# Linear attention and a sparse expert layer on one core: the tile loop written out, and the output product one step later

## Time and profile before

| what | us |
| --- | --- |
| timed runs: median (lowest, highest) of three | 238.04 (237.97, 239.08) |
| profiled execution: span from first to last instruction | 247.9 |
| TensorE busy in the span | 163.8 (66%) |
| VectorE busy | 171.3 (69%) |
| GpSimd busy | 124.1 (50%) |
| ScalarE busy | 99.9 (40%) |

### The profile page before, as it was taken

One profiled execution on the slowest core, in us unless ns is written; L12 is line 12 of the kernel. 1 busy time (PEld: TensorE's weight loads), 2 busy tenths in 40 slices (PEclk: granted clock), 3 DMA queues, 4 the chain that ended last, 5 costly groups with the idle time before them and its releaser, 6 DMA issues.

```text
span 247.9 us, 3949 instructions
## 1 busy us (share of the span) xinstructions
PE 163.8 (66%) x768; PEld 115.4 (47%) x769; DVE 171.3 (69%) x535; ACT 99.9 (40%) x359; POOL 124.1 (50%) x114
## 2 busy tenths in 40 slices
PE   2986966979494886965530004999999889964260
PEld 1444534746352545554420002877687667753140
DVE  0599999999999999999669800655564555540571
ACT  3234444481245822476540001644554454530080
POOL 5763333444057566546577720246466445553380
PEclk9999799797989976897555555999999999999687
DMA  5649100020000101020112243022223222211932
GB/s 149 201 109 408 33 13 3 0 74 11 1 5 17 64 0 43 13 76 23 65 43 86 85 120 81 18 72 78 77 75 85 69 80 65 70 38 64 300 104 73
DMA packets 19198, 18.54 MB, mean 75 GB/s; under 512 B 2944, under 2 KB 16256, under 8 KB 19056
## 3 DMA queue, kind: packets, MB, share of 16 engines
q1 hardware_dynamic: 16880, 13.69, 18.6%
q0 software_dynamic: 2304, 4.69, 5.6%
HBM read 10.60 MB, written 6.73 MB: 70 GB/s over the span
## 4 chain that ended last, share of the span: by engine, by line
PE 30%; issue 26%; DVE 18%; SPq 6%; POOL 6%; DMA 5%; ACT 4%; DVEq 2%; POOLq 0%; ACTq 0%
PE bank L745 8%; DVE prod L1014 5%; PE bank L753 5%; PE bank L736 5%; PE bank L734 3%; POOL zbuf L501 3%; DVE num L1021 3%; PE bank L735 3%; PE bank L571 2%; DMA pl<-both 2%; SPq L421 2%; DVE qk L990 2%; PE bank L725 2%; ACT actT L954 1%; SPq L428 1%
## 5 line engine op out<-in xcount | busy, mean ns | idle before, releaser
L538 POOL DMA_INDIRECT both<-yout,zin x39 | 37.4, 960 | 44.1 <-DVE yout L1295 28.2
L483 POOL TENSOR_TENSOR kv<-v,qk 128x1152 f32<-128x1152 f32 x16 | 34.9, 2180 | 36.2 <-DVE qk L990 32.0
L584 PE MATMUL bank<-kv,C 128*128 128x432 f32 (+1 forms) x96 | 39.8, 556 | 1.9 <-DVE prod L1014 1.8
L501 POOL DMA_INDIRECT zbuf<-rows,slot x32 | 32.1, 1004 | 13.8 <-issue 8.1
L745 PE MATMUL bank<-w_l,actT 128*128 x156 | 25.6, 286 | 7.0 <-ACT actT L954 6.4
L584 PEld LDWEIGHTS bank<-kv,C 128*128 128x128 f32 x96 | 20.2, 227 | 20.3 <-issue 16.1
L1295 DVE COPY yout<-bank 128x128 f32<-128x128 f32 x39 | 11.4, 292 | 24.7 <-PE bank L745 17.0
L745 PEld LDWEIGHTS bank<-w_l,actT 128*128 128x128 f32 x156 | 20.3, 190 | 17.4 <-issue 17.4
L725 PE MATMUL bank<-C,zin 128*128 128x128 f32 x39 | 11.3, 290 | 22.9 <-DMA zin<-zbuf 22.8
L1014 DVE TENSOR_TENSOR prod<-bank,qk 128x432 f32<-128x432 f32 (+1 forms) x48 | 24.4, 547 | 0.5 <-DVE slot L1178 0.5
L1280 DVE TENSOR_TENSOR zin_lo<-bank,zin_hi 128x128 fp32r<-128x128 f32 x39 | 11.4, 292 | 17.5 <-ACT zin_hi L944 14.2
(11 more groups left out here) (152 smaller groups left out, 359.8 us busy)
## 6 DMA issues: line engine op xcount, KB each, us to landing
zin<-zbuf SPq DMA_DIRECT2D x39, 65.0 KB
w_g<-in_gate_w SPq DMA_DIRECT2D x4, 512.0 KB, 6.3
pl<-both SPq DMA_DIRECT2D x8, 256.0 KB, 5.4
xTs<-in_xT SPq DMA_DIRECT2D x16, 64.0 KB, 2.2
w_l<-in_lin_w SPq DMA_DIRECT2D x1, 1024.0 KB, 9.4
zall<-zs SPq DMA_DIRECT2D x4, 256.0 KB
out<-pl SPq DMA_DIRECT2D x8, 128.0 KB, 1.8
both<-yout,zin POOLq DMA_INDIRECT x39
```

The lines of the kernel that those rows point to most:

```text
L483: pool.tensor_tensor(kv[:, s, :].rearrange("p (h e d) -> p h e d", e=HE, d=HD), a, b, ALU.mult).then_inc(kv_done, 1)
L501: pool.indirect_dma_start(zbuf, bass.IndirectOffsetOnAxis(ap=slot_of(g)[:, c:c + 1].bitcast(U32), axis=0), rows_of(g)[:, j, r, :], None)\
L538: pool.indirect_dma_start(both, bass.IndirectOffsetOnAxis(ap=zin[:, b, D + 1:D + 2].bitcast(U32), axis=0), yout[:, b, :], None).then_inc(p ...
L584: pe.matmul(pre_ps[b][:, 0:c1 - c0], const("tri"), kv[:, s, c0:c1], start=True, stop=True)\
```

## The change

The loop of `tiles` and the loops of SyncE and GpSimd over the tiles are written out, with constants as the values waited for. The stages `output` on TensorE and `take` on VectorE get lag 4 in place of 3. `output` also waits until the product of two tiles before, which used the same PSUM bank, has been taken. The expert's number is kept in eight registers in place of four, as it is needed for longer.

```diff
         def tiles(eng, *stages):
-            def step(k, n, rounds=0):
+            def step(k):
                 for lag, stage in stages:
-                    if not isinstance(k, int) or 0 <= k - lag < TILES:
-                        stage(k - lag, (n - lag) % BUFS, rounds + (n - lag) // BUFS)
-
-            for k in range(REST):
-                step(k, k)
-            with eng.Fori(0, ROUNDS) as i:
-                for b in range(BUFS):
-                    step(BUFS * i + (REST + b), REST + b, i)
-            for k in range(TILES, TILES + max(lag for lag, _ in stages)):
-                step(k, k)
+                    if 0 <= k - lag < TILES:
+                        stage(k - lag, (k - lag) % BUFS, (k - lag) // BUFS)
+
+            for k in range(TILES + max(lag for lag, _ in stages)):
+                step(k)
...
-            with sp.Fori(1, ROUNDS) as i:
-                for b in range(BUFS):
-                    k = BUFS * i + b
-                    sp.reg_load(row, tile_r[0:1, bass.ds(k, 1)])
-                    at = sp.snap(row, min_val=0, max_val=SPARE + (NSPARE - 1) * P)
-                    sp.wait_ge(placed[b], 16 * i)
-                    sp.dma_start(zin[:, b, :], zbuf[bass.ds(at, P), :]).then_inc(zin_loaded[b], 16)
-            for k in range(BUFS * ROUNDS, TILES):
-                b = k % BUFS
+            for k in range(BUFS, TILES):
+                rnd, b = divmod(k, BUFS)
                 sp.reg_load(row, tile_r[0:1, k:k + 1])
                 at_row = sp.snap(row, min_val=0, max_val=SPARE + (NSPARE - 1) * P)
-                sp.wait_ge(placed[b], 16 * ROUNDS)
+                sp.wait_ge(placed[b], 16 * rnd)
                 sp.dma_start(zin[:, b, :], zbuf[bass.ds(at_row, P), :]).then_inc(zin_loaded[b], 16)
...
-            with pool.Fori(0, ROUNDS) as i:
-                for b in range(BUFS):
-                    place(BUFS * i + b, b)
-            for k in range(BUFS * ROUNDS, TILES):
+            for k in range(TILES):
                 place(k, k % BUFS)
...
-            expert = [pe.alloc_register(f"expert{b}") for b in range(4)]
+            expert = [pe.alloc_register(f"expert{b}") for b in range(BUFS)]
...
             def output(k, b, rnd):
                 e = expert_of(b)
                 pe.wait_ge(actT_done, k + 1)
+                if k >= 2:
+                    pe.wait_ge(yout_done, k - 1)
...
-            tiles(pe, (0, turn_in), (1, gates), (3, output), (2, turn_act))
+            tiles(pe, (0, turn_in), (1, gates), (4, output), (2, turn_act))
...
-            tiles(ve, (0, rest_zin), (3, take), (1, activate))
+            tiles(ve, (0, rest_zin), (4, take), (1, activate))
```

More of the change, by code:

```diff
@@ L709, in _ @@
             ranks(last)
-            expert = [pe.alloc_register(f"expert{b}") for b in range(4)]
+            expert = [pe.alloc_register(f"expert{b}") for b in range(BUFS)]
             def look_up(k, b):
-                pe.reg_load(expert[b % 4], tile_e[0:1, at(k)])
+                pe.reg_load(expert[b % BUFS], tile_e[0:1, k:k + 1])
             def expert_of(b):
-                return pe.snap(expert[b % 4], min_val=0, max_val=E - 1)
+                return pe.snap(expert[b % BUFS], min_val=0, max_val=E - 1)
             def turn_in(k, b, rnd):
@@ L736, in gates @@
                 pe.matmul(g, zin_lo[:, b % 2, :], hi, start=False, stop=True).then_inc(gate_done, 1)
-                if not isinstance(k, int) or k + 1 < TILES:
+                if k + 1 < TILES:
                     look_up(k + 1, b + 1)
```

## The result

The changed kernel takes 251.53 us (median of four runs, 248.47 to 253.25), the kernel before 238.22 beside it. The ratio is 1.0481, with a 95% interval from 1.0422 to 1.054. The change makes the kernel slower, as was forecast, but by 13.3 us in the medians where 4.2 had been forecast, and 251.53 us lies above the stated range of 236.3 to 243.9. The ratio leaves out runs more than 1.5% above the fastest of their kernel, here 252.3 and 253.25, and the medians take them in, so the two do not divide exactly.

What follows compares the result with a forecast made beforehand. The ring of eight input buffers was to become the bound, four tiles per 6.5 us: stretch 52.0 against 48.0, +4.0, fill -0.45, drain +1.0, exit -0.3, so 238.04 + 4.2 = 242.2 us; range 236.3 to 243.9.

Steps and rivals of the forecast that it cites:

- The mechanism: Input buffers: reload waits for the scatter's landing, lag 4 lengthens the way round, TensorE waits for loads; 1.62 us per tile.
- few breaks: Steps where TensorE's signals come a microsecond late cost the first trace 9.3 us; timed runs were held likelier to have few.
- rival 1: Tiles 6 to 38: late-signal steps occur in timed runs too, so the change gains 1.7 us: 236.3 us; chance 0.27.
- the ring's turn: Way round the eight input buffers: 6.5 us besides whole steps, so after the change four tiles per 6.5 us.
- The load: Reload of an input buffer by SyncE: taken as 1.5 us, last packet plus its signal, between 0.9 and 1.83.
- The bound above: Ceiling of the input load, 1.83 us, from the first of eight loads in flight together; it would give +6.8 us.
- The restart: TensorE after waiting for a load: taken as a quiet step, 0.81 us transpose to output product, 0.64 to the take.
- The stretch before: Tiles 6 to 38 of the kernel before: 32 steps of 1.47 us plus 1.0 for loops, 48.0 us.
- Drain: Last tiles: scatters by GpSimd 1.30 us apart would make the end 1.0 us longer without breaks.
- fill: First steps: one output product moves out of step 3, saving 0.45 us.
- loops: Three ways back between tiles 6 and 38, 0.33 us each: writing out saves 1.0 us, plus 0.3 for the exit.
- The fourth rival: Input buffers: scatter and load both at about 2.15 us, so 7.03 us per four tiles, 246.4 us; chance 0.04.

Runs made afterwards that it cites:

- Experiments 1 to 6: Ratios to before: lag 4 only 1.0499; written out, lag 3, 8/7/6 buffers 1.0072/1.0535/1.1576; changed kernel with 12 buffers 0.99, or reloading before scatter lands 0.9917.
- experiment 2: The changed kernel with lag 3 instead of 4, loops still written out and added wait kept: 240.08 us, 1.0072 of before.
- experiment 0: The kernel before, unchanged, profiled a second time: span 238.7 us, timed at 240.61 us (one run).
- experiments 1 and 4: The kernel before with only lag 4, added wait and eight registers: 250.3 us; the changed kernel with lag 3 and 7 buffers: 250.74 us.
- experiment 4: The changed kernel with lag 3 and 7 buffers instead of lag 4 and 8: 250.74 us, 1.0535 of before.

## Why the prediction was right and wrong

**The mechanism was right.** The reload is bound to the scatter's landing, the lag lengthens the way round by a step, and TensorE waits at the input's transpose. Experiments 1 to 6 show it, and no other part of the change is shown to cost anything; the 0.7% of experiment 2 stays open.

**That the timed runs have few breaks was right,** though the evidence was thin: two numbers of like size, 9.3 and 9.9 us. No run of before reached 242 us, and experiment 0 has no break, so nothing speaks for rival 1. For the reason I gave, a profiler that delays signals, nothing speaks either; that the guess on the timed runs came true is in part luck.

**The step that failed: the ring's turn was mis-sized, 6.5 us against 7.17.** Term by term, by the chain of the changed kernel:

- The load: 1.5 against 1.87. I read a strip of the DMA engines up to the last packet and allowed next to nothing for the signal behind it. The bound above, 1.83, lay nearer. This is 0.37.
- The restart: I let a step that had waited run as a quiet one. From transpose to output product it takes 0.99 instead of 0.81, and its product 0.1 longer. From the transpose to the take it is 162.87 - 161.08 = 1.79 us where I had 0.81 + 0.64 = 1.45. This is 0.34. I had the 0.1 in the earlier trace rows and used it for the breaks, not for the ring.
- Scatter (2.23) and take to issue (0.30 + 0.03 + 0.74 = 1.07) were as read.

Eight turns are 57.4 us instead of 52.0: 5.4 us.

**Slow transfers had no term.** 61.66 - 57.4 = 4.3 us are turns longer than 7.17. Three reloads on the chain are 0.6, 1.7 and 1.4 us over 1.84, 3.7 in all, and nearly all of that is lost; the turn at the lower clock behind one of them is the other 0.9. The size differs from run to run: with the same spare steps experiments 1 and 4 have 60.47 and 60.32 in the stretch. With time to spare in the ring such a transfer costs little, as in the kernels with ten and twelve buffers; with none it adds nearly its whole lateness. I had a first scatter-to-reload of 3.04 in the earlier trace rows and put it only in a rival. Why a transfer is slow, no run shows.

**The stretch before was too cheap, by 2.2 us in the profile.** I took 48.0 us for tiles 6 to 38 of before; experiment 0 has 50.16. With the true turn the ring of before has 8 x 1.47 - 3 x 1.47 - (7.17 - 0.34) = 0.5 us to spare, not 0.9, so slow transfers reach it too. In experiment 0 the scatter and load of tile 8's buffer were 1.57 late together, some 1.05 more than there was to spare, and the step from tile 7 to tile 8 took 162.09 - 159.56 = 2.53 us, 1.05 over the quiet one. That is what 10 or 12 buffers win. This error had the other sign. Together: +5.4 + 4.3 - 2.2 = +7.5 on the +4.0 forecast for the stretch, the 11.5 measured. How the 13.3 us of the timed medians divide is not shown to that detail: the profiled run of before was one of its longer ones, and the 2.2 may be less in a usual run.

**Drain, fill and loops.** The drain grew from 6.97 to 7.95 us, +1.0 as predicted, by scatters 1.26 apart (I had 1.30). The transpose of tile 6 came 8.6 us after that of tile 0 instead of 9.8, but that is no measure of the change: it is 8.78 in the first profile of before, and over all profiles with at least 8 buffers 8.78 to 9.79 with lag 3 and 8.62 to 9.21 with lag 4, 0.4 apart in the mean where I had 0.45. The three ways back of the loop, 1.0 forecast, are steps 0.33, 0.27 and 0.23 longer in experiment 0, 0.8 together; no gain from writing them out is seen in the timed runs.

**The fourth rival came nearest.** It priced both transfers at about 2.15, an estimate by the Trainium skill (DMA: Bandwidth & Descriptors, anatomy of one DMA), and its turn of 7.03 us gave 246.4 us. I gave it 0.04 as the trace seemed to have the load at 1.5. The measured scatter is 2.2 and the load 1.8 to 1.9 in both kernels, 0.3 below that price, and it was my reading of the strip that was off. The Trainium skill gives that price for transfers issued by GpSimd, as the scatter is, and I had used it for SyncE's load as well. That its turn is so near to 7.17 is in part luck: the load priced 0.3 too high stood in for the restart, which it lacked too. The range ended at 243.9 because I had set the ceiling of the load, which alone gave +6.8 in all, aside.

## What to carry to other kernels

A lag in a software pipeline is paid for in buffers: count the way round from the release of a buffer, signals and landings of both transfers included, and set it against buffers minus lag. In a ring that binds, the spread of the transfers adds to their mean, so leave a microsecond or two to spare before asking for overlap elsewhere. And when a profile's span is longer than the timed runs, take a second profile before explaining what the first one shows.

## What had not been expected of the hardware

- Behind a wait of 1.99 us in the middle of dense matmuls TensorE's granted clock fell to its lower level (0.50 from 211 to 214 us), and behind waits of 0.78 and 1.30 us it stayed full. The length of the wait does not decide it alone. In experiment 4 a wait as long left the clock at 1.00 from 190 to 198 us:

```profile
193.82 0.33 PE L710 MATMUL bank<-C,zin 128*128 128x128 f32 x1 [2.00 <-DMA zin<-zbuf]
```

- Reloads of the same 65 KB took 1.8 us mostly, but 2.43, 3.56 and 3.22 us now and then in one profile. Scatters took 2.2 us mostly, but 3.31 in experiment 0 and 4.48 in experiment 4.
- One execution of the kernel before was about 9 us longer than its fellows, with TensorE's signals a microsecond late some eleven times. Neither its second profile nor that of the changed kernel shows such breaks. Its cause stays open.
